# Node pass of a graph network kernel: POOL's block sum moved ahead of its row-map transfers

## What is computed

```python
h = jnp.maximum(_layernorm(x, axis=-1), 0.0)
x = x + _L0_gnn_ref(h, edge_index, edge_attr_16, ...)   # 5 attention layers, with a bias each
h = jnp.maximum(_layernorm(x, axis=-1), 0.0)
x = x + _L1_gnn_ref(h, edge_index, edge_type_2, ...)
h = jnp.maximum(_layernorm(x, axis=-1), 0.0)
x = x + _L2_gnn_ref(h, edge_index, L2_gnn_W, L2_gnn_b)  # gelu
h = jnp.maximum(_layernorm(x, axis=-1), 0.0)
x = x + _L3_gnn_ref(h, edge_index, edge_type_4, ...)
```

## Time and profile before

| | |
|---|---|
| runs of the kernel | 5289.17 us median of 3 (5286.49 to 5291.38) |
| span of the profiled execution, first to last instruction | 5284.5 us |
| mean granted clock of PE over the span | 0.880 of full speed |
| busy: PE, DVE, ACT, POOL | 4281.1, 4007.8, 3358.8, 3254.8 us |
| node pass: first and last power (L479) on POOL | 107.6 and 1576.3 us |
| instructions of POOL in the whole kernel | 2905 |

### The profile page before, as it was taken

One profiled execution on the slowest core, in us unless ns is written; L12 is line 12 of the kernel. 1 busy time (PEld: TensorE's weight loads), 2 busy tenths in 40 slices (PEclk: granted clock), 3 DMA queues, 4 the chain that ended last, 5 costly groups with the idle time before them and its releaser, 6 DMA issues. The chain is left out here.

```text
span 5284.5 us, 101919 instructions
## 1 busy us (share of the span) xinstructions
PE 4281.1 (81%) x28013; PEld 3707.5 (70%) x28013; DVE 4007.8 (76%) x15157; ACT 3358.8 (64%) x9065; POOL 3254.8 (62%) x2905
## 2 busy tenths in 40 slices
PE   4899999999976978969969958776895858869575
PEld 4777777778865867858858847644775847757475
DVE  5799999999976766767757767787676959859765
ACT  2788887888855866847847847643873537758400
POOL 2888888878877727637457367222761257566277
PEclk6999999999988989989989979855997979989755
DMA  3999876665645636636636546487773759847332
GB/s 92 187 219 217 220 218 212 222 219 206 212 150 125 143 85 133 135 77 142 128 90 141 110 107 142 110 246 225 169 153 90 196 141 248 236 114 132 74 94 85
DMA packets 1107280, 825.56 MB, mean 156 GB/s; under 512 B 209510, under 2 KB 1068202, under 8 KB 1106396
## 3 DMA queue, kind: packets, MB, share of 16 engines
q1 hardware_dynamic: 1026800, 690.47, 48.7%
q0 software_dynamic: 77040, 128.08, 12.0%
q10 hardware_dynamic: 2880, 0.50, 0.1%
HBM read 374.78 MB, written 448.11 MB: 156 GB/s over the span
## 5 line engine op out<-in xcount | busy, mean ns | idle before, releaser
L805 POOL DMA_INDIRECT gat_G<-table,k_src_row x980 | 1071.7, 1094 | 316.6 <-issue 282.5
L1598 ACT ACTIVATE gat_Gw<-gat_G,gat_al 128x128 f32<-128x128 f32 x1960 | 618.5, 395 | 89.0 <-DVE gat_al L1423 89.0
L1454 DVE SCALAR_TENSOR_TENSOR gat_Gw<-gat_own,gat_al,gat_Gw 128x128 f32<-128x128 f32 x1960 | 555.3, 344 | 70.5 <-ACT gat_Gw L1598 70.3
L1715 PE MATMUL gat_psG<-gat_ends_at,gat_Gw 128*128 128x128 f32 x3920 | 536.4, 281 | 42.3 <-DVE gat_Gw L1454 42.2
L1743 PE MATMUL gat_psZ<-gat_aggT,t_gat_wh 128*128 128x256 f32 x1960 | 525.5, 391 | 16.5 <-ACT gat_hT L1624 16.1
L1715 PEld LDWEIGHTS gat_psG<-gat_ends_at,gat_Gw 128*128 128x128 f32 x3920 | 491.9, 197 | 53.3 <-DVE gat_Gw L1454 50.1
L635 PEld LDWEIGHTS nodes_psR<-t_ident_v,nodes_hTl 128*128 128x128 f32 x3168 | 435.3, 193 | 106.0 <-issue 1.8
L635 PE MATMUL nodes_psR<-t_ident_v,nodes_hTl 128*128 128x132 f32 x3168 | 450.5, 279 | 0.0
L479 POOL TENSOR_TENSOR nodes_rstd<-nodes_var,k_half 128x14 f32<-128x14 f32 x140 | 367.7, 2626 | 116.0 <-DVE nodes_var L546 116.0
L1624 ACT ACTIVATE gat_hT<-gat_psZ,t_gat_bias 128x256 f32<-128x256 f32 x490 | 231.6, 473 | 266.4 <-PE gat_psZ L1744 263.4
L1743 PEld LDWEIGHTS gat_psZ<-gat_aggT,t_gat_wh 128*128 128x128 f32 x1960 | 338.6, 193 | 57.9 <-ACT gat_aggT L1605 18.7
(11 more groups left out here) (668 smaller groups left out, 12635.5 us busy)
## 6 DMA issues: line engine op xcount, KB each, us to landing
table<-nodes_rows SPq DMA_DIRECT2D x660, 198.0 KB
table<-nodes_n SPq DMA_DIRECT2D x396, 192.0 KB
gat_own<-table SPq DMA_DIRECT2D x490, 132.0 KB
table<-gat_rows SPq DMA_DIRECT2D x392, 132.0 KB
nodes_x<-in_x SPq DMA_DIRECT2D x132, 192.0 KB
out<-nodes_x_out SPq DMA_DIRECT2D x132, 192.0 KB
gat_G<-table,k_src_row POOLq DMA_INDIRECT x980
hgt_q<-enter_q SPq DMA_DIRECT2D x98, 144.0 KB, 2.2
```

The costliest lines, as they stand in the source:

```text
L805: eng.indirect_dma_start(to, None, table, bass.IndirectOffsetOnAxis(ap=index, axis=0)).then_inc(sem, 16)
L1454: ins = eng.scalar_tensor_tensor(Gw[:, i % RS, t, h, :], own[:, i % RO, t, 0:D], al[:, g % 2, 1, a:a + 1], Gw[:, i % RS, t, h, :], ALU.mul ...
L1598: ins = eng.activation(Gw[:, i % RS, t, h, :], G[:, i % RG, t, 0:D], ACT.Copy, scale=al[:, g % 2, 0, a:a + 1])
L1715: mm = eng.matmul(o[:, h * P:(h + 1) * P], Gw[:, i % RS, t, h, :], ends_at[:, i % RE, t, :], start=True, stop=True)
```

## The change

In POOL's list of a step, the sum `xb` stands behind the power and the slot gathers and ahead of the three row-map transfers, in place of behind these. No instruction is added or removed, and no wait.

```diff
                     if is_slots(k + 2):
                         gather_slots(k + 2)
+                    if is_block(k):
+                        with_bias(k)
                     for what, c in steps[k * per:(k + 1) * per]:
                         if what == "put":
                             eng.indirect_dma_start(K.row_of, bass.IndirectOffsetOnAxis(ap=K.node_tm[:, c:c + 1], axis=0),
                                                    K.slot_row_tm[:, c:c + 1], None, bounds_check=K.rows - 1,
                                                    oob_is_err=False).then_inc(s.row_put, 16)
                         else:
                             if c == 0:
                                 eng.wait_ge(s.row_put, 16 * C)
                             gather(eng, K.row_of, K.src_tm[:, c:c + 1], K.src_row[:, c:c + 1], s.row_got)
-                    if is_block(k):
-                        with_bias(k)
                     if N <= k < N + 8:
                         c = (k - N) * 25
```

## The result

**The result.** The kernel with the sum between gathers and map transfers took 5366.97 us (median of 4 runs, 5359.95 to 5373.08), the kernel before on the same chip 5290.27 (median of 4, 5286.49 to 5300.94). The ratio is 1.0132, 95% interval 1.0118 to 1.0147: slower by 76.7 us. Forecast were 5324 us, that is +35, and a range of 5278 to 5369: the time lies inside the range, near its upper end, and the change is more than twice the forecast one. The profiled execution of the changed kernel took 5370.25 us, its span 5368.5, 84.0 more than the 5284.5 of before.

The account below looks back on a forecast made before the run. The cycle POOL list, `xb`, L538, variances, power was taken as the bound, the PE and ACT loop next. Gather blocks 0, clock falls +31, blocks without gathers +6, block 130 -2.6: +35, so 5324 us; range 5278 to 5369.

Parts of the forecast that it names:

- The stop: In blocks with slot gathers the moved sum holds DVE's fifth norm tile until 0.10 us behind the sum's end.
- the first rival: In blocks with slot gathers the sum stops DVE only from its own start on: 5280 to 5286 us, chance 0.17.
- The block without a fall: A block with slot gathers and no clock fall takes 11.03 us, with PE's turn at 6.55 and L621 at 9.81.
- POOL's list: In blocks with slot gathers POOL keeps up, its transfers ending at 10.3 us, 11.6 at worst; no cost taken.
- The sign that I gave: POOL's wait before the power would be 0.2 to 0.6 us, listed among what would show the forecast.
- The falls: PE's clock falls after its wait for `n2` in gather blocks: 19 falls of 1.65 us, +31 us, bounds 0 and 55.
- 4 blocks in 10 at 0.9 or more: Share of the 84 gather blocks where PE's wait for `n2` reaches 0.9 us, used to count falls; upper bound 7 in 10.
- Blocks without gathers: In 31 blocks the sum right behind the power holds L584; 9.76 us a block against 9.56, +6 us, bounds 0 and 16.
- Block 130: This block, with the sum already ahead of its third map transfer, loses its stop: 12.39 to 9.76 us, -2.6 us.
- The clock stays: Rival: in gather blocks the stop moves in front of PE without clock falls; +3, 5293 us, chance 0.18.
- The fourth tile: Rival: the fourth norm tile is stopped in gather blocks, with falls in 2 blocks of 5; 5369 us, chance 0.12.
- `xb` did not wait for DVE: Rival: `xb` waits for DVE and not the reverse, making POOL's list 0.6 us longer; 5290 us, chance 0.05.

Follow-up runs that it names:

- Experiment 1: Changed kernel with the sum behind the first map transfer in blocks that issue slot gathers, last in the others: 5297.49 us, ratio to the kernel before 1.0005.
- experiment 5: Changed kernel with the sum put back behind the map transfers in the 84 blocks that issue slot gathers: 5286.1 us, ratio to the kernel before 1.0006.
- experiment 3: Changed kernel with two more matmuls on PE ahead of its wait for `n2` in blocks 12 to 95: 5300.33 us, ratio to the kernel before 1.001.
- experiments 4 and 8: Changed kernel with zero fills of 128x384 in place of the sum: one fill (4) 5283.91 us, ratio 0.997; two fills (8) 5269.98 us, ratio 0.9979.
- experiment 6: Kernel before with the sum straight behind the power, ahead of the gathers, in blocks that issue gathers and the last block: 5280.82 us, ratio 0.9998.
- experiment 2: Changed kernel with the sum behind the second map transfer in blocks with slot gathers, last in the others: 5299.2 us, ratio to the kernel before 1.0005.

## Why the prediction was right in kind and wrong in size

**The stop.** Right. The fifth tile is held, as block 130 of before had shown for the sixth, and not only from the sum's own start: it should have ended at 546.42 (546.08 + 0.34) and the sum's row begins at 546.75. The gather that runs at that moment doesn't hold it: beside the same gather, with no sum behind it, six tiles take 1.62 us in block 36 of before. That refutes the first rival, which is what the Trainium skill's rule (SBUF — State Buffer, "SBUF: two separate sides") gives when it is read on the rows' starts. By the rows the stop ends as the rule says, with POOL's instruction; its beginning is ahead of the row.

**The block without a fall.** Forecast: `n2` at 6.50, PE at 6.55, L621 at 9.81, block 11.03. In block 37 PE turns at 548.27 - 541.62 = 6.65, L621 starts at 9.90, and the block takes 11.14. The tenth of a microsecond is 8 us over 84 blocks.

**POOL's list.** I took nothing for it, and it came out at the very edge. The second map write is held to 2.08 beside L602 to L613, and block 38's power starts 0.11 behind the last transfer's end (551.66 + 0.99 = 552.65) with no wait shown. DVE's variances end at 552.66, so both are ready together. Experiment 1 shows the list as the bound, up to block 64. The sign that I gave, a wait of POOL of 0.2 to 0.6 before the power, did not come as such: up to block 64 it is mostly 1.75 behind a fall and 0.11 else.

**The falls: the step that failed.** "I take 4 blocks in 10 at 0.9 or more" was the wrong term; it was 10 in 10. PE's wait is 1.10 or more in every gather block, and 1.24 to 1.40 in 78 of the 84. The other factor, 8 falls in 14 such waits, was nearly right: 84 x 8/14 = 48, and 42 came. That it was so near is luck: the 14 were waits of 0.90 to 1.58 in no order, and the falls that came are nearly every second block. The cost of one, 1.65, was right (12.75 - 11.13 = 1.62). With 10 in 10 the sum would have been 84 x 11.03 + 2.3 - 928.9 + 48 x 1.65 + 6 - 2.6 = +83; measured +77.

Why I had the wait too small can be read in the trace of before. I started from 0.70 (block 36) and let it grow to 0.9 or 1.0 in some blocks. The 0.70 is a point on a climb, as PE's turns in the three blocks behind it show, with the windows of blocks 38 and 39 (columns as above):

```profile
521.84 0.33 PE L627 MATMUL nodes_psB<-k_ident,nodes_n 128*128 128x128 f32 x1 [0.77 <-DVE nodes_n L523]
...
532.88 0.33 PE L627 MATMUL nodes_psB<-k_ident,nodes_n 128*128 128x128 f32 x1 [0.85 <-DVE nodes_n L523]
...
543.91 0.33 PE L627 MATMUL nodes_psB<-k_ident,nodes_n 128*128 128x128 f32 x1 [0.93 <-DVE nodes_n L523]
```
```profile
527.64:538.67 11.03, 10.14 (x74) 8.71 (x73) 10.46 (x38) 8.91 (x23) 9.00 (x7) 1.00 0.93 233
538.67:550.03 11.36, 10.43 (x69) 9.68 (x69) 9.13 (x38) 8.62 (x21) 8.98 (x7) 0.85 0.81 223
```

PE gains 0.08 us a block on DVE, its loop of 10.95 against blocks of 11.03; at 0.93 the clock falls, the fall sets PE back, and the climb starts again. (Behind block 69 the blocks of before take 10.94 to 10.98, the wait stays at 0.00 or 0.01 in the rest of the stretch, and no fall comes.) Where such a climb ends, the trace of before shows as well, in its first blocks, and I passed over it: the turn waits 1.14, 1.22 and 1.24 us in blocks 12 to 14. The turn and the window of block 13:

```profile
256.11 0.33 PE L627 MATMUL nodes_psB<-k_ident,nodes_n 128*128 128x128 f32 x1 [1.22 <-DVE nodes_n L523]
```
```profile
250.88:261.92 11.04, 9.82 (x74) 8.63 (x73) 10.47 (x38) 9.06 (x23) 9.00 (x7) 1.00 0.94 183
```

The wait is all the time in which PE idles there, 11.04 - 9.82 = 1.22, as it is in block 36 of the changed kernel, 12.74 - 11.44 = 1.30. So with blocks of 11.03 a wait that nothing sets back had to come out near 1.2, and the prediction itself says that nothing would: "the wait is there again in the next block". Block 130 showed it for this very stop, 1.44, and I used that row for the tile and not for the wait. The windows of blocks 38 and 39 show what a fall costs before: block 39 is 0.33 longer, since L538 is no longer held (0.17 in place of 1.5) and gives the rest back. In the changed kernel nothing gives it back: DVE, POOL and PE all shift by 1.62, and the next block finds PE's wait as long as before.

**Blocks without gathers.** Right: 300.51 - 296.32 = +4.2 against +6, 9.69 a block against 9.76; experiment 5 shows the same alone. The sum right behind the power (1570.00 above) holds L584, by about 0.5. **Block 130:** -2.7 against -2.6.

**The rivals.** "The clock stays" (5293) is what experiment 3 makes of the change by keeping PE at work. The fourth tile was held in one gather block (32); 5369, given to that case (with 55 us for the falls, where 34 x 1.65 is 56), is near the measured time for another reason: luck. `xb` did not wait for DVE: its longest is 1.04.

## What to carry to other kernels

A moved instruction stops its neighbours at the new place as it did at the old; price it from a block of the old trace that already has the new order, and take from there every row, the waits behind the stop too. A stop ahead of a stage that also waits for PE hides a dip of PE's clock; the same stop in front of PE makes the dips and hides none. Ask of a wait in a periodic trace whether it is a level or a climb that something resets: look at it in five blocks in a row, not in one. Where it can end is the length of the block less the busy time of the engine.

## What the runs showed of the hardware

- A POOL instruction holds DVE's norm tiles (scale and shift of 128x128) from before its own row begins: the fifth tile of the changed kernel is late from 546.42 on at the latest, the sum's row starts at 546.75, right behind the second gather. Plain fills hold them as well (experiments 4 and 8). For that the Trainium skill has a rule (SBUF — State Buffer, "Who interferes with whom"): scaling instructions can run in a mode that takes the ports shared with POOL, against any POOL instruction; an instruction with two inputs in SBUF meets only POOL's reads, and one with a single input, outside that mode, doesn't meet POOL. The held norms under fills and the unheld statistics of experiment 6 agree with it; why the stop begins early was not tried.
- The effect seems to go the other way too. An indirect transfer that POOL issues while DVE runs its three sums of 128x384 (L602 to L613) takes up to 2.36 us in place of 1.0 and ends at a fixed distance behind them: 549.27 + 2.08 = 551.35 in block 37 of the changed kernel, 0.88 behind L613's end (550.47). In blocks 16 to 63 this distance has a median of 0.87 in the kernel before and of 0.89 in experiment 1, where the longer transfer set the bound. That the sums are the cause is read from this timing; no run took them away.
- In the two climbs shown the granted clock fell after PE's wait of 0.93 us (before) and of 1.03 (experiment 1), and stayed up in the blocks ahead, at 0.85 and 0.89; at about 0.57 in each block it stayed up for 63 gather blocks. One wait by itself doesn't decide: before, the clock stayed up after 0.93 in blocks 67 and 68 and after 1.22 in block 13, and in block 130, with a wait of 1.43 to 1.45 in four kernels, it fell in two (before, experiment 2) and not in the others (experiments 1 and 6). With a wait of 1.3 to 1.4 in each block it fell in nearly every second one. What makes it every second one stays open.
